# One block of a residual network and a mixture of experts: where four output-bias additions, two roundings and two products stand in their ticks

## The reference, cut to what matters

```python
out = silu(scale * _layer_norm(x, gamma, beta) + shift)
out = out @ W_in + b_in
out = silu(scale * _layer_norm(out, gamma, beta) + shift)
x2 = out @ W_out + b_out + x
h = gelu(x2 @ Wi[e] + bi[e], approximate=False)      # 512 x 2048
r = h @ Wo[e] + bo[e] + x2                            # 512 x 512
y = (r - mean(r)) * rsqrt(var(r) + LN_EPS) * gamma[e] + beta[e]
```

## Time and profile before

| | before |
|---|---|
| median of three runs | 1809.83 us |
| the profiled execution, its time | 1809.61 us |
| its span | 1807.7 us |
| PE busy | 1752.9 us, 97% |
| DVE busy | 1481.3 us, 82% |
| ACT busy | 1055.6 us, 58% |
| POOL busy | 86.7 us, 5% |
| granted clock of TensorE, mean | 0.999 |
| matmuls of 128x256 (L724) | 2352, 0.28 us each, one every 0.12 us |

### The profile page before, as it was taken

How to read it: one execution, slowest core, us unless ns; L and a number is a source line. 1 busy time by engine, 2 the same in 40 slices (tenths; PEclk the granted TensorE clock), 3 DMA queues, 4 the chain that set the end, 5 groups by cost and what they waited for, 6 DMA issues and landing times.

```text
span 1807.7 us, 25797 instructions
## 1 busy us (share of the span) xinstructions
PE 1752.9 (97%) x8947; PEld 1482.3 (82%) x8947; DVE 1481.3 (82%) x2471; ACT 1055.6 (58%) x1699; POOL 86.7 (5%) x137
## 2 busy tenths in 40 slices
PE   9999999999999999999999999999999999999998
PEld 6888888878888788887888878788787887878887
DVE  7987879888798887978879788797887988878685
ACT  5756565565655665556665556645566555665543
POOL 1000000000000000000000000000000000000000
PEclk9999999999999999999999999999999999999999
DMA  6332423324233232332323323233241332313241
GB/s 251 96 97 85 143 74 111 118 70 132 85 109 108 92 112 83 120 108 84 126 66 120 109 94 120 63 123 104 94 132 62 120 108 84 130 62 120 82 135 63
DMA packets 71555, 189.57 MB, mean 105 GB/s; under 512 B 13955, under 2 KB 18051, under 8 KB 71300
## 3 DMA queue, kind: packets, MB, share of 16 engines
q1 hardware_dynamic: 62642, 183.95, 31.0%
q10 hardware_dynamic: 8786, 3.99, 1.1%
HBM read 171.10 MB, written 16.81 MB: 104 GB/s over the span
## 4 chain that ended last, share of the span: by engine, by line
PE 79%; DVE 10%; ACT 7%; issue 2%; DMA 1%; SPq 0%; DVEq 0%; ACTq 0%; POOL 0%
PE out_acc L635 32%; PE hid_ps L635 32%; PE blk_ps L724 14%; ACT work L893 2%; ACT x L920 2%; DVE x_turned L1362 2%; DVE h_lo L1100 1%; PE blk_ps L635 1%; DVE g_lo L1100 1%; ACT L876 1%; DVE wo_lo L1100 1%; DVE wi_lo L1100 1%; ACT L893 1%; DMA cond_a<-in_cond_w 1%; ACT g_hi L880 1%
## 5 line engine op out<-in xcount | busy, mean ns | idle before, releaser
L635 PE MATMUL hid_ps<-x_hi,wi_hi 128*128 128x512 f32 x1020 | 398.2, 390 | 0.0
L635 PE MATMUL hid_ps<-x_lo,wi_hi 128*128 128x512 f32 x1020 | 398.2, 390 | 0.0
L635 PE MATMUL hid_ps<-x_hi,wi_lo 128*128 128x512 f32 x1020 | 396.8, 389 | 0.0
L635 PE MATMUL out_acc<-wo_hi,g_hi 128*128 128x512 f32 x1012 | 393.7, 389 | 0.0
L635 PE MATMUL out_acc<-wo_lo,g_hi 128*128 128x512 f32 x1012 | 393.7, 389 | 0.0
L635 PE MATMUL out_acc<-wo_hi,g_lo 128*128 128x512 f32 x1012 | 393.6, 389 | 0.0
L876 ACT ACTIVATE g_sb<-hid_ps,bi_sb 128x512 f32<-128x512 f32 x256 | 175.7, 686 | 268.9 <-PE hid_ps L635 268.5
L1100 DVE TENSOR_TENSOR g_lo<-g_sb,g_hi 128x512 fp32r<-128x512 f32 x253 | 173.1, 684 | 158.7 <-ACT g_hi L880 155.9
L834 ACT ACTIVATE wo_hi<-stage 128x512 fp32r<-128x512 f32 x253 | 159.8, 632 | 147.1 <-PE out_acc L635 147.0
L1100 DVE TENSOR_TENSOR wo_lo<-stage,wo_hi 128x512 fp32r<-128x512 f32 x253 | 173.7, 687 | 65.1 <-ACT wo_hi L834 64.9
L635 PEld LDWEIGHTS hid_ps<-x_hi,wi_lo 128*128 128x128 f32 x1020 | 191.5, 188 | 40.7
(11 more groups left out here) (202 smaller groups left out, 2450.8 us busy)
## 6 DMA issues: line engine op xcount, KB each, us to landing
stage<-in_expert_w SPq DMA_DIRECT2D x256, 512.0 KB, 3.5
x<-in_xT SPq DMA_DIRECT2D x64, 256.0 KB, 3.3
out_y<-x_turned SPq DMA_DIRECT2D x63, 256.0 KB, 2.5
rows<-in_expert_rows SPq DMA_DIRECT2D x16, 512.0 KB, 4.5
mv_all<-mv_dram ACTq DMA_DIRECT2D x30, 128.0 KB, 3.3
affine_sb<-in_affine SPq DMA_DIRECT2D x3, 512.0 KB, 9.6
w_raw<-in_W SPq DMA_DIRECT2D x2, 512.0 KB, 5.8
w_raw<-in_W_in SPq DMA_DIRECT2D x4, 256.0 KB, 9.4
```

What stands on the lines that cost most here:

```text
L635: last = pe.matmul(dst, w[wp], xs[xp], start=start and i == 0, stop=stop and i == 2)
```

## The change

Five things, all of them in the order of the work; no arithmetic is added or left out.

1. The output bias (`bo_part`) of batches 2 to 15 moves from ACT's tick 0 to the ends of ACT's ticks 2 and 3, two in each. (Tick 16 of a batch is tick 0 of the next one, tick 18 its tick 2.)
2. In DVE's split of both layers, rest A12 moves ahead of the differences T1 and T3.
3. In the first layer, ACT rounds only A11 and A12 in tick 1. S3, S2 and S1 are rounded in tick 2, and the first take of bank 0 follows them; all of these stand behind gelu and `wi_hi` and ahead of `wo_hi`.
4. In the first layer, rest S1 and the first take of bank 1 move, in DVE's tick 2, ahead of `g_lo`, `wi_lo` and `wo_lo` (behind `r_evac`).
5. On PE, S2_T2 (bank 0) is made before S3_T3 (bank 1) in ticks 3 and 13. All waits that count products go by the new place (`TURN_OF`).

```diff
-            W_OUT: (), BO: (16,), X_OUT: (-2,), X_BACK: (-2,), A_OUT: (6,), A_BACK: (7,), X_BOUT: (6,)}
+            W_OUT: (), BO: (18, 18, 19, 19), X_OUT: (-2,), X_BACK: (-2,), A_OUT: (6,), A_BACK: (7,), X_BOUT: (6,)}
...
-                         W_OUT: (13, 13, 14, 14), BO: (15,), X_OUT: (2,), X_BACK: (3,), A_OUT: (),
+                         W_OUT: (13, 13, 14, 14), BO: (15,) * DC, X_OUT: (2,), X_BACK: (3,), A_OUT: (),
...
+TURN_OF = (0, 1, 3, 2, 4, 5, 6)
...
-PRODUCTS_AT = ({2: (0, 1), 3: (2, 3), 4: (4,), 5: (5, 6)}, {12: (0, 1), 13: (2, 3), 14: (4,), 15: (5, 6)})
+PRODUCTS_AT = ({2: (0, 1), 3: (3, 2), 4: (4,), 5: (5, 6)}, {12: (0, 1), 13: (3, 2), 14: (4,), 15: (5, 6)})
...
+def products_until(b, which, i):
+
+    return PRODUCTS * sevens_before(b, which) + TURN_OF[i] + 1
...
-                if b == FIRST_SEVEN and i in (S3_T3, S1_T1, S4_B22):
+                if b == FIRST_SEVEN and i == S2_T2:
                     pe.wait_ge(s_sumlo[which], 4)
...
# ACT, each tick
                 if FIRST_PAIR < k + 1 < STEPS and not wi_first(k):
                     wi_hi_part(k + 1)
+                for b, which in sevens_due(k, TAKE_AT[0]):
+                    if not which:
+                        for i in (S3_T3, S2_T2, S1_T1):
+                            rounded(b, which, i)
+                        take_in(b, 0)
...
-                for b, _ in block_a_due(k, BO):
-                    for m in range(DC):
-                        bo_part(b, m)
...
                 for b, which in sevens_due(k, SPLIT_AT):
-                    for i in range(WAVE):
+                    for i in (A11_B11, A12_B21, S3_T3, S2_T2) if which else (A11_B11, A12_B21):
                         rounded(b, which, i)
                 for b, which in sevens_due(k, TAKE_AT[0]):
-                    if not which:
-                        take_in(b, 0)
-                    rounded(b, which, S1_T1)
+                    if which:
+                        rounded(b, which, S1_T1)
...
+                for b, m in block_a_due(k, BO):
+                    bo_part(b, m)
...
# DVE, each tick
+                for b, which in sevens_due(k, TAKE_AT[0]):
+                    if not which:
+                        rest(b, which, S1_T1)
+                        take_1_in(b, 0)
                 if wi_first(k):
                     wi_lo_part(k + 1)
...
                 for b, which in sevens_due(k, SPLIT_AT):
                     rest(b, which, A11_B11)
+                    rest(b, which, A12_B21)
                     combine(b, which, T1)
                     combine(b, which, T3)
-                    rest(b, which, A12_B21)
                     rest(b, which, S3_T3)
...
-                    else:
-                        rest(b, which, S1_T1)
-                        take_1_in(b, 0)
```

More of the change, by code:

```diff
@@ L947, in rounded @@
                 if i >= WAVE:
-                    act.wait_ge(s_product, PRODUCTS * before + i - WAVE + 1)
+                    act.wait_ge(s_product, products_until(b, which, i - WAVE))
                 elif before:
@@ L957, in take_in @@
                 before = sevens_before(b, 0)
-                act.wait_ge(s_product, PRODUCTS * before + (A11_B11, S2_T2, S1_T1, S4_B22)[n] + 1)
+                act.wait_ge(s_product, products_until(b, 0, (A11_B11, S2_T2, S1_T1, S4_B22)[n]))
                 if n == 0:
@@ L1267, in take_1_in @@
                 before = sevens_before(b, 0)
-                dve.wait_ge(s_product, PRODUCTS * before + (A12_B21, S1_T1, A22_T4)[n] + 1)
+                dve.wait_ge(s_product, products_until(b, 0, (A12_B21, S1_T1, A22_T4)[n]))
                 dve.wait_ge(s_take0, 4 * before + (1, 3, 2)[n])
@@ L1281, in take_0_out @@
                 before = sevens_before(b, 1)
-                dve.wait_ge(s_product, PRODUCTS * before + (A11_B11, S2_T2, S1_T1, S4_B22)[n] + 1)
+                dve.wait_ge(s_product, products_until(b, 1, (A11_B11, S2_T2, S1_T1, S4_B22)[n]))
                 dve.wait_ge(s_bout, DC * (b - FIRST_SEVEN + 1))
@@ L1288, in take_1_out @@
                 before = sevens_before(b, 1)
-                dve.wait_ge(s_product, PRODUCTS * before + (A12_B21, S3_T3, A22_T4)[n] + 1)
+                dve.wait_ge(s_product, products_until(b, 1, (A12_B21, S3_T3, A22_T4)[n]))
                 dve.wait_ge(s_take0, 4 * before + (1, 3, 2)[n])
```

## The result

| | before | after |
|---|---|---|
| median | 1810.16 us (4 runs, 1809.48 to 1810.61) | 1762.28 us (4 runs, 1761.95 to 1763.42) |
| profiled execution, its time and span | 1809.61, 1807.7 us | 1762.18, 1760.2 us |
| PE busy | 1752.9 us, 97% | 1749.2 us, 99% |
| DVE busy | 1481.3 us, 82% | 1466.8 us, 83% |

The ratio is 0.9737 (95% interval 0.972 to 0.9754): 47.9 us less. The forecast was 1759.4, in a range of 1754 to 1767.

A forecast was written before the change was run, and what follows sets the result against it. PE, busy 97%, bounds the kernel, and only its gaps can change. 49.3 us (13 batches) plus 1.8 (first batch) less 0.7 (`up(12)`) gives 50.4 off 1809.61: 1759.2, median 1759.4 us, range 1754 to 1767.

The forecast's parts named there:

- What bounds the kernel: PE, busy 97%: its work plus its gaps at the seven-product matmuls; a new order can win 57.2 us together.
- Part 1: ACT's tick 0: without the output bias gelu comes 2.02 us earlier, so product A11's 1.75 us stall goes.
- the margin of 0.1 us: At product A11: its remainder is ready for 1050.79, PE would start without a wait at 1050.89.
- the 0.05 that I had put down: At product A11: 0.05 us per batch left for the weight load starting ahead of the matmul, bounds 0 and 0.5.
- Part 2: DVE's split: A12's 0.39 us stall goes; a new wait of about 0.4 us per batch comes before `down` in tick 2.
- Parts 3 to 5: Head of tick 3: S3's 1.37 us stall goes, no other PE wait follows, DVE level again by tick 6.
- the list of signs: Waits that would show steps wrong: A11 0.3 us or more, `up(12)` or `up(3)` above 0.2, any in tick 13 to 15.
- the new wait: Before the first `down` tile of tick 2: about 0.4 us per batch, paid once, bounds 0 and 1.0.
- the term for `up(12)`: Second layer, tick 10: `wi_lo` 0.49 us later makes a draw; 0.05 us per batch, 14 times, 0.7 us.
- No new wait: Rival: the wait before `down` does not come; about 1754 us, chance 0.15.
- Part of the first stall stays: Rival: ACT's chain gains about 1.2 us, not 2.02, so A11 still waits; about 1768 us, chance 0.22.
- The statistics through DRAM: Rival: tick 13's swap delays the next batch's statistics, then A11; slower than before, chance 0.03.

The follow-up runs named there:

- A12 back: The changed kernel with rest A12 back behind T1 and T3 in DVE's split of both layers: 1761.14 us, ratio 0.9732.
- one `r_evac` in the gap: The changed kernel with the first of four `r_evac` moved into DVE's 0.70 us wait for ACT's rounding of S3, first layer: 1754.36 us, ratio 0.9691.
- `r_out` early and the stores first: The changed kernel with `r_out` at the head of DVE's tick 4 and SyncE's stores of y ahead of block 7's load: 1764.07 us.
- one pair of kernels: The changed kernel with `r_out` at the head of DVE's tick 4, stores of y behind block 7's load or ahead: 1826.11 and 1764.07 us.
- the other: The changed kernel with an `r_evac` moved into DVE's wait, late second-layer rounding and early `r_out`, stores behind the load or ahead: 1822.18 and 1755.21 us.
- the early `r_out`: The changed kernel with `r_out` at the head of DVE's tick 4 and nothing else: 1826.11 us, ratio 1.0084.

## Why the prediction was right

- **What bounds the kernel.** Right. Of the 57.8 us that PE lost before, 57.4 lay in the three places of the earlier trace rows and in the two stalls of the first batch with seven products, and the forecast had 57.2 from batch distances.
- **Part 1.** Right, by what limits it: 2.02 us and not 2.55, from tick 9. The distance is 5.03 us again. Alone it won 26.7 us, and taking it back cost 27.5. A11 was on time in every batch, so the margin of 0.1 us held; the 0.05 that I had put down was not lost, 0.65 us too much.
- **Part 2.** Right: A12's wait went, and a wait of `down` for `r_evac` came, 0.38 us later than due, where 0.40 was worked out. Two experiments bind it to DVE's chain: with A12 back it is gone, with one `r_evac` in the gap too. The sentence of the Trainium skill that the prediction draws on (VectorE: DVE Perf Modes, section The DRAIN you can't avoid) would have made it 0.65 us by the prediction's working; the 6.11 us distance follows the 0.60 us of independent instructions. But the same section of the Trainium skill goes on to say that a next instruction which is not held starts earlier. The 0.60 us between instructions that are drawn 0.68 us long agree with that. The prediction left it out, so its contrast between the Trainium skill and the rows was too sharp.
- **Parts 3 to 5.** Right for the head of tick 3: no wait there. Parts 4 and 5 are each needed: without them 9.2 and 3.6 us come back. Part 3 was not tried by itself. Wrong in what follows: that no other wait of PE comes of it, and that DVE is level with PE by tick 6. The loss came at `up(11)`, which the list of signs did not name.
- **The size.** The sum was 2.9 us too good (1762.28 against 1759.4). Mis-sized are two terms. First, the new wait: 6.4 us and not 13 x 0.40 + 0.3 = 5.5, because a wait costs PE a slower second matmul too, 0.08 us each time; I had counted this for the stalls of before by taking batch distances, and not for the new one. That is 0.9. Second, the term for `up(12)`, 0.7 us, measured 2.1 with `up(11)`, 1.4 more. The draw at `up(12)` was itself worked out well: in the kernel with `r_out` early and the stores first, `wi_lo` ends 0.15 us before `up(12)` starts and nothing is lost. What made DVE later than that is above all the wait for the stores of y, 15.4 us in place of 1.6, which no step of mine had looked for: I moved `r_out` earlier with DVE's queue and left the stores' landing out. Another 0.3 us lies in the head of the kernel (one start there is at 122.44 and not at 122.11), with the code there unchanged. Less the 0.65 of part 1 this makes some 2.0 of 2.9 us; the rest I have not traced. That the forecast came this near is in part luck: the 0.65 us that part 1 was charged too much hides as much of what was charged too little.
- **The rivals.** No new wait: excluded by the trace; its time, about 1754, is what the kernel with one `r_evac` in the gap took (1754.36). Part of the first stall stays: excluded, A11 shows no idle. The statistics through DRAM: no wait of that kind shows.

## What to carry to other kernels

When the bound engine waits at several places of one period, take for each the chain that releases it and ask what stands in that chain only by order; then add up the new order to the next instruction that the bound engine will need, for that is where it waits next. A gap in which a second engine waits for a third is the right place for work that is due soon: one `r_evac` there was worth more than the reordering of A12. And a step brought forward has to be followed through every queue that it releases or holds, the DMA queue's own too: here stores behind a load that waited for DVE cost 62 us in one pair of kernels and 67 in the other.

## What the runs showed of the hardware that I had not expected

After a wait of PE of 2.4 us shown (2.53 to 2.57 lost between starts) the granted clock fell in 9 of 14 batches of the kernel with the early `r_out`, in the other five not; the lengths of the waits do not tell the two apart. Stretches of this kernel around one that fell (columns: stretch, its length, busy time and count of PE, weight loads, DVE, ACT, POOL, then the granted clock, the DMA share and GB/s):

```profile
440.00:448.00 8.00, 5.75 (x25) 4.43 (x24) 5.82 (x9) 6.71 (x10) 0.00 (x0) 1.00 0.46 155
448.00:452.00 4.00, 3.85 (x10) 3.09 (x11) 3.27 (x7) 1.48 (x3) 0.00 (x0) 0.57 0.63 208
452.00:460.00 8.00, 8.00 (x48) 7.08 (x48) 7.10 (x12) 5.54 (x10) 0.00 (x0) 1.00 0.22 66
```

For most of 4 us the clock was at its lower level of 1.2 GHz, matmuls of 512 columns followed each other 0.43 us apart in place of 0.23, and about 1.6 us were lost over the wait itself, against 0.12 to 0.16 in the batches where the clock stayed. In the kernel before, waits of 1.75 us (1.91 lost between starts) did this in none of 13 batches (granted clock of the whole run 0.999, against 0.992 there).
